# Two products of the gate and up stage placed one group earlier, with rank work placed later on ACT and DVE

## What is computed

```
x = x + x @ w0[id0[b]].T                                  # layer 0, one of 16 matrices per batch
x = x + x @ W.T + 2 * gated low-rank terms of 8 experts   # layer 1, top 2 of a router
x = x + x @ W2.T + bias + 0.5 * (x @ A2[id2[b]]) @ B2.T   # layer 2, rank 32
gate = x @ Wg.T + 0.5 * (x @ Ag[id3[b]].T) @ Bg[id3[b]].T # layer 3, rank 16, 1376 columns
up   = x @ Wu.T + 0.5 * (x @ Au[id3[b]].T) @ Bu[id3[b]].T
act  = silu(gate) * up
x = x + act @ Wd.T + 0.5 * (act @ Ad[id3[b]].T) @ Bd[id3[b]].T
```

## Time and profile before

| | |
|---|---|
| median of 3 runs | 288.58 us (288.47 to 288.65) |
| profiled execution, its own time | 288.6 us |
| span of the profiled execution | 286.8 us |
| PE busy | 279.4 us (97% of the span) |
| PEld busy | 231.2 us (81%) |
| DVE busy | 227.5 us (79%) |
| ACT busy | 158.5 us (55%) |
| POOL busy | 45.7 us (16%) |
| mean granted clock of PE | 0.999 of full speed |

### The profile page before, as it was taken

How to read it: one execution, slowest core, us unless ns; L and a number is a source line. 1 busy time by engine, 2 the same in 40 slices (tenths; PEclk the granted TensorE clock), 3 DMA queues, 4 the chain that set the end, 5 groups by cost and what they waited for, 6 DMA issues and landing times.

```text
span 286.8 us, 4499 instructions
## 1 busy us (share of the span) xinstructions
PE 279.4 (97%) x1573; PEld 231.2 (81%) x1573; DVE 227.5 (79%) x341; ACT 158.5 (55%) x256; POOL 45.7 (16%) x67
## 2 busy tenths in 40 slices
PE   7899999999999999999999999999999999999993
PEld 7567878888888778888888888888888888888883
DVE  0698897894746999989686785785789999799990
ACT  2688672512425269775746646646667849952110
POOL 1000000000714502514244044044000000000000
PEclk9999999999999999999999999999999999999999
DMA  6999954007603040030270350330291500000043
GB/s 199 371 401 395 400 181 112 0 0 237 204 0 81 22 125 25 10 139 0 65 228 5 100 193 2 110 111 0 73 336 69 152 0 0 0 2 0 0 181 113
DMA packets 19447, 33.28 MB, mean 116 GB/s; under 512 B 2528, under 2 KB 11232, under 8 KB 19040
## 3 DMA queue, kind: packets, MB, share of 16 engines
q1 hardware_dynamic: 19136, 32.47, 33.2%
q10 hardware_dynamic: 288, 0.52, 0.6%
HBM read 30.89 MB, written 2.10 MB: 115 GB/s over the span
## 4 chain that ended last, share of the span: by engine, by line
PE 95%; DMA 2%; DVE 1%; SPq 1%; issue 0%
PE bank L1617 12%; PE bank L1618 12%; PE bank L1619 12%; PE bank L1494 6%; PE bank L1496 6%; PE bank L1495 6%; PE bank L1757 6%; PE bank L1759 6%; PE bank L1760 6%; PE bank L1599 4%; PE bank L1454 3%; PE bank L1471 2%; PE bank L1478 2%; PE bank L1742 2%; DMA w_raw<-in_w 2%; PE bank L1480 2%
## 5 line engine op out<-in xcount | busy, mean ns | idle before, releaser
L619 ACT ACTIVATE part<-bank 128x512 f32<-128x512 f32 x48 | 28.3, 595 | 44.8 <-PE bank L1619 34.7
L1218 DVE TENSOR_TENSOR part<-bank,part 128x512 f32<-128x512 f32 x44 | 29.2, 683 | 1.4 <-PE bank L1599 1.4
L1143 DVE SCALAR_TENSOR_TENSOR bgu_st<-bgu_st,lo_rows,bgu_raw 128x512 fp32r<-128x512 f32 x22 | 17.3, 824 | 12.1 <-ACT bgu_st L619 12.1
L967 DVE TENSOR_TENSOR w_hl<-w_raw,w_hl 128x512 fp32r<-128x512 f32 x31 | 20.0, 687 | 5.6 <-ACT w_hl L619 5.6
L619 ACT ACTIVATE w_hl<-w_raw 128x512 fp32r<-128x512 f32 x31 | 18.6, 622 | 6.1 <-DMA w_raw<-in_w 6.0
L601 POOL TENSOR_TENSOR s_tmp<-wgu_raw 128x256 f32<-128x256 f32 x11 | 8.4, 762 | 80.7 <-DVE wc_up L967 38.8
L1617 PE MATMUL bank<-xb,wc_gate 128*128 128x512 f32 x48 | 18.9, 394 | 0.0
L1619 PE MATMUL bank<-xb,wc_gate 128*128 128x512 f32 x48 | 18.9, 394 | 0.0
L1618 PE MATMUL bank<-xb,wc_gate 128*128 128x512 f32 x48 | 18.8, 392 | 0.0
L1599 PEld LDWEIGHTS bank<-t_st,bgu_st 128*128 128x128 f32 x88 | 14.7, 188 | 2.8 <-DVE t_st L1208 0.3
L619 ACT ACTIVATE xb<-x_f 128x512 fp32r<-128x512 f32 x14 | 8.8, 626 | 13.4 <-DVE x_f L1088 9.4
(11 more groups left out here) (227 smaller groups left out, 792.1 us busy)
## 6 DMA issues: line engine op xcount, KB each, us to landing
wgu_raw<-in_wgu SPq DMA_DIRECT2D x11, 512.0 KB, 4.4
bgu_raw<-in_bgu SPq DMA_DIRECT2D x40, 128.0 KB, 2.7
w_raw<-in_w SPq DMA_DIRECT2D x16, 256.0 KB, 10.9
w_raw<-in_w SPq DMA_DIRECT2D x3, 1024.0 KB, 6.8
w_raw<-in_w SPq DMA_DIRECT2D x6, 512.0 KB, 10.4
wd_raw<-in_wd SPq DMA_DIRECT2D x4, 704.0 KB, 5.9
x_f<-in_xT SPq DMA_DIRECT2D x6, 256.0 KB, 10.1
bd_raw<-in_bd SPq DMA_DIRECT2D x8, 128.0 KB, 2.8
```

The costliest lines, as they stand in the source:

```text
L619: return act.activation(dst, src, ACT.Copy)
L967: return dve.tensor_tensor(dst, src, hi.bitcast(F32), ALU.subtract)
L1143: return dve.scalar_tensor_tensor(out=st, in0=st.bitcast(F32), scalar=lo_rows16[:, 0:1], in1=raw, op0=ALU.mult, op1=ALU.add)
L1218: dve.tensor_tensor(dst[:], bank[4 * (n % 2) + b][:], dst[:], ALU.add).then_inc(c_added, 1)
```

## The change

Three lists of calls are written in another order; nothing is added or removed.

On PE, `p1(1)` and `p2(1)` move from behind `thin3(1)` to directly behind `p2(0)`, ahead of `sum_ranks(0)`. On ACT, `xt_high(2)`, both remaining splits of step 1's weights and `copy_part(1, 0)` move ahead of `t3_high(0)`. On DVE, both `wc_low` of step 1 and `xt_low(2)` move ahead of `t3_low(0)` and `bgu_low(0, 1)`.

```diff
@@ block.scalar
             t3_copy(0)
             xt_high(1)
             copy_part(0, 0)
+            xt_high(2)
+            wc_high(1, 1)
+            wc_high(1, 2)
+            copy_part(1, 0)
             t3_high(0)
             copy_part(0, 1)
-            xt_high(2)
             t3_copy(1)
-            wc_high(1, 1)
-            wc_high(1, 2)
             bgu_high(0, 1)
-            copy_part(1, 0)
             xt_high(3)
@@ block.vector
             form_t(2)
             form_t(3)
-            t3_low(0)
-            bgu_low(0, 1)
             for part_of in (1, 2):
                 wc_low(1, part_of)
             xt_low(2)
+            t3_low(0)
+            bgu_low(0, 1)
             xt_low(3)
             t3_low(1)
@@ block.tensor
             p2(0)
             pe.wait_ge(t3_sel_step, 1 + 2 * HB)
             pe.wait_ge(x_sum, number(2, 1, C - 1) + 1)
+            p1(1)
+            p2(1)
             sum_ranks(0)
             p5(0)
             thin3(1)
-            p1(1)
-            p2(1)
             p6(0)
             sum_ranks(1)
```

## The result

The changed kernel takes 293.25 us (median of 4 runs, 291.60 to 294.67) against 288.52 us, a ratio of 1.0163 with an interval of 1.0136 to 1.0190. It is slower, as forecast, but by 4.7 us and not by 3.2, and 293.25 lies outside the range of 290.8 to 292.7.

A forecast was written before the change was run, and what follows sets the result against it. The prediction took PE to bound the kernel, with no slack behind the change. A 3.26 us gap plus 0.1 for an exposed load less 0.18 at lora_y(0) gave 288.6 + 3.2 = 291.8 us, range 290.8 to 292.7.

The forecast's parts named there:

- What bounds the kernel: PE holds 95% of the last chain; from 118 us nearly no slack, so any gap on PE reaches the end.
- The chain on ACT and DVE: From form_t(2)'s end at 107.70, rank pieces queue behind moved instructions; t3_low(0) ends at 115.00, a 3.26 us PE gap.
- the forecast's own count: Gap ahead of sum_ranks(1), counted from the slot where PE's next matmul would have begun: 111.79 to 115.05, 3.26 us.
- the 121.7: Time in us at which lora_y(0) is due on PE after the gap; t3_low(1) ends by 119.5, so its wait goes.
- the sum: On PE from lora_y(0) to the end: 3.26 + 0.1 - 0.18 = 3.2 us later, giving 291.8 us.
- By itself this part is worth nothing: PE's move of p1(1) and p2(1), 2.76 us of matmuls: p6(0) still ends where it did.
- the first rival: Clock falls in PE's gap ahead of sum_ranks(1): 2.0 us more, 293.8 us; chance 0.09.
- A gap of 3.3 us is shorter, though not by much: PE's gap compared with the 3.7 us from the last matmul to the clock's fall at the trace's end.
- The price of the fall: Half pace on PE for some 4 us of work, read from warm-up matmuls: about 2 us lost.
- the exposed load: First weight load of sum_ranks(1) on PE, exposed behind the gap: 0.1 us.
- Not slower: Whole kernel: no gap at sum_ranks(1), 288.3 to 288.6 us; chance 0.04.

The follow-up runs named there:

- e7: Changed kernel with xt_low(3) too moved ahead of t3_low(0) on DVE, for a longer gap; 296.23 us, ratio 1.0283.
- e8: Kernel before with t3_low(1) ahead of xt_low(3) on DVE, so that lora_y(0) no longer waits for it; 287.68 us, ratio 0.9981.
- e9: Changed kernel with DVE back in its old order, ACT and PE in the new one; 291.00 us, ratio 1.0087.
- e5: Changed kernel with xt_low(2) back behind t3_low(0) and bgu_low(0, 1) on DVE; 289.88 us, ratio 1.0052.
- e6: Changed kernel with POOL starting form_s(2) only when t3_low(0) is done; 292.44 us, ratio 1.0140.
- e1: Changed kernel with PE back in its old order, only ACT and DVE in the new one; 292.64 us, ratio 1.0131.
- e2: Kernel before with only PE's move of p1(1) and p2(1), ACT and DVE in the old order; 290.40 us, ratio 1.0069.
- e4: Changed kernel run again without a change, for how often the clock falls; 292.63 us, ratio 1.0151.
- e10: Kernel of e8 with thin3(1) directly behind sum_ranks(0) on PE, ahead of p5(0); 288.58 us, ratio 1.0003.
- e3: Changed kernel with 20 matmuls of unused result between p6(0) and sum_ranks(1) on PE; 291.83 us, ratio 1.0114.

## Why the prediction was right and wrong

**What bounds the kernel** was right: PE's gaps carry through to the end. e7 shows it with a gap of 5.7 us, e8 from the other side.

**The chain on ACT and DVE** was right in all its terms. Forecast and trace: `xt_high(2)` 107.74 and 107.58, `t3_high(0)` 110.4 and 110.28, `xt_low(2)` 1.74 and 1.76 us, `t3_low(0)` 112.98 and 112.78, the gap 3.26 and 3.36 us in the forecast's own count (3.19 in the profile's). One slip changed nothing: `lora_y(0)` is due 6.7 us after `sum_ranks(1)`, not after `lora_w(0)` as written (118.50 - 111.79), and the 121.7 that follows is right. e9 splits the gap by engine, e5 and e6 by instruction. Without a fall of the clock the time is 3.2 us over each level of the kernel before (e1), the sum to a tenth. The 288.6 that the forecast built on is of the upper level; that the two exist wasn't known, and a lower run without a fall takes 291.0 (e1).

**"By itself this part is worth nothing"**, of PE's move, was right within the changed kernel (e1 has the same gap without it), and would have been wrong alone: with ACT's old order it costs 2.3 us (e2).

**The step that failed is the first rival's**: "A gap of 3.3 us is shorter, though not by much." I had one place at which the clock fell, 3.7 us behind PE's last matmul at the end of the trace, took that as the idle time that a fall needs, gave the rival 9 in 100, and ended the range at 292.7, below its 293.8. It was one sample of something that varies, and I took it for a threshold. The ends of the other traces, which have the same idle stretch, show how much: there the clock fell 2.1 us (e4) to 4.2 us (e2) behind the end of the last matmul, 2.6 us in the changed kernel, and in four traces (e1, e6, e9, e10) not within the 4.3 us that were left. Behind the gaps of 3.2 us the clock fell in 11 of 15 runs, behind those of 2.6 us in 4 of 6. In the trace after it fell 0.7 us behind PE's return, which I had not thought of at all: that the work is back before the clock has fallen doesn't prevent the fall. A gap that comes near the one sample should have had an even chance, and the forecast a range up to 294. The rule of the Trainium skill that I set beside the row (TensorE: Matmul & The Clock Gate, Part 1, "What's actually happening": an idle PE falls back to half its clock) described what happened; I had let a row with one sample outvote it.

**The price of the fall** was set at 2.0 us and is 1.5 to 1.8 (293.50 to 293.58 against 291.78 us in e1, 292.74 and 292.81 against 291.24 in e6). It was read from the pace of the warm-up matmuls; the profile's granted clock is 1.00 in those windows, so that no row there shows a low clock itself. In the trace after, 1.07 + 0.57 + 2.53 us for `sum_ranks(1)`, `lora_w(0)` and `p3(0)`, where the kernel before has 0.80 + 0.32 + 1.39, is 1.66 us more, with 0.1 of it the exposed load. The rows of the kernel before for this, behind `sum_ranks(1)` at 111.79:

```profile
112.59 0.48 PE L1599 MATMUL bank<-t_st,bgu_st 128*128 128x256 f32 x2
112.91 0.40 PE L1617 MATMUL bank<-xb,wc_gate 128*128 128x512 f32 x1
...
114.30 0.40 PE L1617 MATMUL bank<-xb,wc_up 128*128 128x512 f32 x1
```

**Not slower**: no run of the changed kernel came within 2.9 us of the kernel before's highest in its series.

## What to carry to other kernels

Where one engine is packed, work out for every instruction that is moved ahead on another engine what it is moved ahead of, and when the packed engine will ask for that; the splits that were moved ahead on ACT and DVE, and that nobody was waiting for yet, cost 3.2 us here because they then stood ahead of the rank pieces, which PE was due to need. Count a gap on PE of the size of those here (2.6 us and more) not at its own length alone but with the clock's fall on top, which came in 20 of 26 runs and was half as much again behind the gap of 3.2 us; gaps of 1.5 us and less came without it, and between 1.5 and 2.6 us nothing was measured. If such a gap can't be closed, matmuls into an unused half of a bank keep the clock up (1.4 us here), and if it can be split into several small ones, these cost their own sum without the clock's part (2.3 us for three in e2, 2.5 in e9); in the profile's count of idle time that sum looks some 0.5 us smaller than it is.

## What the runs showed of the hardware that I had not expected

The granted clock fell at very different distances from the end of the last matmul before the gap: 2.3 us in e6, while PE was still idle, 3.1 us in e1, 3.2 in e7, 3.4 in e4, and 3.9 us in the trace after (whose last row of 0.4 us begins at 111.35), 0.7 us into new work. Why it varies, no run here shows. It stayed low for 3.4 us in all of these but e7, and for 6.9 us there. Gaps of 1.50 us (e5), 1.17 us (e9) and 0.95 us (e3) never brought it down, in 17 runs.

The idle end of each trace shows the same spread. These are windows of PE in the changed kernel, in e4 and in e10, in this order; the last matmul's rows end at 287.10, 287.25 and 282.41 us:

```profile
289.00:290.00 1.00, 0.00 (x0) 0.85 0.41 152
289.00:290.00 1.00, 0.00 (x0) 0.68 0.59 215
286.00:286.70 0.70, 0.00 (x0) 1.00 0.00 0
```

The clock fell at about 289.7 and 289.36 us, 2.6 and 2.1 us behind the last matmul, and in e10 it was still at full speed at the end of the span, 4.3 us behind it.

POOL's sums cost a DVE subtraction that starts just behind the first of them 0.54 us (1.76 against 1.22 us), and the rank pieces, which read PSUM, nothing (2.01 us in both cases). It holds the other way round too: POOL's second sum (line 602) took 1.70 us in the changed kernel, where `xt_low(2)` ran beside it, and 0.72 us in e5, where the rank pieces did. Delaying POOL is enough to get the 0.54 us on DVE back (e6).
